# Token rows transposed by VectorE and DRAM transfers in a macaron block; sine part joined, floor moved to GpSimd

## The reference

```python
x = x + 0.5 * ffn(layernorm(x))
x = x + attn(layernorm(x))         # softmax of 0.5 + 0.2*sigmoid(qk) + 0.15*tanh(qk) + 0.1*relu(qk), over 1024 keys
x = x + 0.5 * ffn(layernorm(x))
# in ffn, for each of its 2 layers:
h = shift_token(x)                 # upper 64 features come from the token before
qkv = h @ wqkv                     # 128 -> 3 x 512
q = l2norm(q) * qs; k = l2norm(k) * ksc
q, k = rotary_xpos(q, k)           # q*cos*scale + rotate_half(q)*sin*scale
o = local_attention(q, k, v)       # windows of 64, this window and the last
x = x + o @ wo
h = layernorm(shift_token(x)) * lg + lb
a, g = split(h @ w1 + b1)
x = x + (a * gelu(g)) @ w2 + b2
```

## Time and profile before

| | |
|---|---|
| median of 3 runs | 3134.05 us (3133.75 to 3137.78) |
| the profiled execution | 3130.48 us |
| its span in the trace | 3128.7 us, granted TensorE clock 0.993 |
| TensorE matmul busy | 3019.2 us (97%) |
| VectorE busy | 2676.7 us (86%) |
| ScalarE busy | 2224.1 us (71%) |
| GpSimd busy | 1676.7 us (54%) |
| DMA queues | 107.23 MB, mean 34 GB/s |

### The profile page before, as it was taken

How to read it: one execution, slowest core, us unless ns; L and a number is a source line. 1 busy time by engine, 2 the same in 40 slices (tenths; PEclk the granted TensorE clock), 3 DMA queues, 4 the chain that set the end, 5 groups by cost and what they waited for, 6 DMA issues and landing times.

```text
span 3128.7 us, 84476 instructions
## 1 busy us (share of the span) xinstructions
PE 3019.2 (97%) x31009; PEld 2182.5 (70%) x31009; DVE 2676.7 (86%) x6052; ACT 2224.1 (71%) x5488; POOL 1676.7 (54%) x1000
## 2 busy tenths in 40 slices
PE   6999999999999999989999699999999999999999
PEld 3777777666777777656777477777766677777766
DVE  6999999678888888768999599999966888888865
ACT  4888888436888887328889388888853688888832
POOL 6888886115666665541000588888621466666610
PEclk9999999999999999999999899999999999999999
DMA  4111112101111111100000011111211111111211
GB/s 117 33 35 34 33 38 51 45 20 31 33 36 33 36 43 42 46 8 1 1 1 1 18 35 35 34 33 40 45 47 22 31 33 36 33 36 40 46 39 51
DMA packets 136855, 107.23 MB, mean 34 GB/s; under 512 B 80937, under 2 KB 102402, under 8 KB 136450
## 3 DMA queue, kind: packets, MB, share of 16 engines
q1 hardware_dynamic: 136450, 101.83, 14.4%
HBM read 12.67 MB, written 4.19 MB: 5 GB/s over the span
## 4 chain that ended last, share of the span: by engine, by line
PE 88%; DVE 8%; issue 2%; ACT 2%; DMA 0%; SPq 0%; DVEq 0%; ACTq 0%
PE psum L1171 13%; PE psum L1045 10%; PE psum L1148 7%; PE psum L1184 7%; PE psum L1195 7%; PE psum L1215 6%; PE psum L1102 6%; PE psum L1071 5%; PE psum L1136 4%; PE psum L1416 3%; PE psum L1229 3%; PE psum L1242 3%; PE psum L1392 3%; PE psum L1092 3%; PE psum L1402 2%
## 5 line engine op out<-in xcount | busy, mean ns | idle before, releaser
L420 POOL TENSOR_TENSOR rnorm<-ssq_floor,neg_half 128x16 f32<-128x16 f32 x256 | 746.7, 2917 | 659.8 <-DVE qkr L741 626.4
L495 ACT ACTIVATE shared<-psum,neg_max 128x128 f32<-128x128 f32 x2048 | 594.3, 397 | 24.5 <-DVE neg_max L717 24.5
L425 POOL TENSOR_TENSOR qk_cos<-qk_cos,qk_sin 128x1024 f32<-128x1024 f32 x256 | 607.8, 2374 | 0.0
L1171 PE MATMUL psum<-wqkv,hT 128*128 128x512 f32 x1024 | 533.9, 605 | 21.6 <-DVE qk_sin L702 9.7
L702 DVE TENSOR_TENSOR qk_sin<-psum,sin 128x256 f32<-128x256 f32 x1024 | 382.0, 414 | 90.9 <-ACT sq L502 89.9
L516 ACT COPY shared<-psum 128x512 f32<-128x512 f32 x256 | 150.0, 586 | 358.5 <-PE psum L1136 358.5
L708 DVE TENSOR_TENSOR qk_cos<-psum,cos 128x512 f32<-128x512 f32 x512 | 348.7, 682 | 55.1 <-ACT sq L502 54.9
L554 ACT ACTIVATE shared<-psum,b1g 128x512 f32<-128x512 f32 (+1 forms) x192 | 131.3, 686 | 351.7 <-PE psum L1045 349.6
L1195 PEld LDWEIGHTS psum<-wo,shared 128*128 128x128 f32 x2048 | 267.0, 192 | 139.5 <-issue 139.2
L502 ACT ACTIVATE sq<-psum 128x512 f32<-128x512 f32 x512 | 335.0, 654 | 30.9 <-PE psum L1171 30.9
L1045 PE MATMUL psum<-shared,w1g 128*128 128x512 f32 (+1 forms) x768 | 345.8, 593 | 7.2 <-DVE shared L807 5.3
(11 more groups left out here) (131 smaller groups left out, 6580.2 us busy)
## 6 DMA issues: line engine op xcount, KB each, us to landing
vprev<-v SPq DMA_DIRECT2D x512, 130.0 KB, 2.3
shared<-Y SPq DMA_DIRECT2D x32, 256.0 KB
shared<-Y SPq DMA_DIRECT2D x32, 254.0 KB
X<-in_L_attn_x SPq DMA_DIRECT2D x8, 512.0 KB, 6.9
out<-X SPq DMA_DIRECT2D x8, 512.0 KB, 3.6
wqkv<-in_L_ffn_wqkv SPq DMA_DIRECT2D x4, 768.0 KB, 4.5
w<-in_L_ffn_w SPq DMA_DIRECT2D x4, 341.0 KB
wo<-in_L_ffn_wo SPq DMA_DIRECT2D x4, 256.0 KB, 4.8
```

Of the source, the lines that this page charges most:

```text
L420: nc.gpsimd.tensor_tensor(rnorm[:], ssq_floor[:], neg_half[:], ALU.pow).then_inc(rnorm_ready, 1)
L425: nc.gpsimd.tensor_tensor(both, both, qk_sin[:, t.m % 2, :], ALU.add).then_inc(sum_ready, 1)
L495: last = nc.scalar.activation(probs[:, c * P:(c + 1) * P], bank(3 + i, (c % 4) * P, (c % 4 + 1) * P), ACT.Exp, bias=neg_max[:, c:c + 1])
L1171: nc.tensor.matmul(bank(i), hT[:, t.m * P:(t.m + 1) * P], wqkv[:, i * INNER:(i + 1) * INNER], start=True, stop=True).then_inc(qk_psum, 1)
```

## The change

For the tiles 0 to 4 of each layer nothing changes in how they come into hT. From tile 5 on TensorE and ScalarE no longer take part. VectorE transposes the 128x128 tile of Y in sixteen squares of 32, each in its place, into one of two buffers (`token_blocks`, for tile s+7 in slot s, after the moments). SyncE stores the buffer to one of four places in DRAM (tile s+6, first in slot s) and loads the squares from there into their right places in hT with four transfers of 32 partitions (tile s+5, next in slot s); both stand ahead of the `vprev` copies. TensorE's first query projection waits for these loads (semaphore `blocks_in`).

Besides, VectorE's sine part is one instruction over both halves with the halves read in reverse order, so that a tile counts 4 rotary steps instead of 6, and the floor of the sums goes from VectorE to GpSimd, ahead of its power. The wait of `scores` for hT falls away.

```diff
+def late_count(t):
+    return t.L * (64 - EARLY) + t.row - EARLY
...
+            def store_blocks(t):
+                k = late_count(t)
+                sp.wait_ge(blocks_ready, k + 1)
+                wait(sp, blocks_in[k % 4], 64 * (k // 4))
+                sp.dma_start(blocks_out[k % 4], blocks[:, k % 2, :]).then_inc(blocks_stored[k % 4], 16)
+
+            def load_blocks(t):
+                k = late_count(t)
+                sp.wait_ge(blocks_stored[k % 4], 16 * (k // 4 + 1))
+                wait(sp, v_psum, before(t, MT - 1))
+                squares = blocks_out[k % 4].rearrange("(b i) (j c) -> i b j c", i=SQUARE, c=SQUARE)
+                for j in range(P // SQUARE):
+                    lo = t.m * P + (1 if j * SQUARE >= HALF else 0)
+                    sp.dma_start(hT[j * SQUARE:(j + 1) * SQUARE, lo:lo + P].rearrange("i (b c) -> i b c", c=SQUARE),
+                                 squares[:, :, j, :]).then_inc(blocks_in[k % 4], 16)
...
             def local_slot(L, s):
+                if t := late_tile(L, s + 6):
+                    store_blocks(t)
+                if t := late_tile(L, s + 5):
+                    load_blocks(t)
                 if t := tile_at(L, s + 3):
                     wait(sp, v_ready, before(t, 0))
...
             def root(t):
-                wait(pool, floor_ready, before(t, 0))
+                wait(pool, ssq_ready, before(t, 0))
+                wait(pool, rnorm_ready, before(t, 1))
+                nc.gpsimd.tensor_scalar(ssq_floor[:], ssq[:], 1e-24, None, ALU.max).then_inc(floor_ready, 1)
+                pool.wait_ge(floor_ready, t.n + 1)
                 wait(pool, qkr_ready, before(t, 1))
...
-                if s >= 0 and (t := tile_at(L, s + 5)):
-                    tokens(t)
...
-                for e in range(2):
-                    lo = e * (DH // 2)
-                    nc.vector.tensor_tensor(
-                        y[:, :, e, :], x[:, :, 1 - e, :],
-                        sin[:, t.m, i:i + 1, lo:lo + DH // 2].to_broadcast([P, HEADS, DH // 2]),
-                        ALU.mult).then_inc(rot_ready, 1)
+                part = sin[:, t.m, i, :].rearrange("p (e d) -> p e d", e=2)
+                nc.vector.tensor_tensor(y, x[:, :, ::-1, :],
+                                        part.unsqueeze(1).to_broadcast([P, HEADS, 2, DH // 2]),
+                                        ALU.mult).then_inc(rot_ready, 1)
...
-                wait(dve, ssq_ready, before(t, 0))
-                wait(dve, rnorm_ready, before(t, 1))
-                nc.vector.tensor_scalar_max(ssq_floor[:], ssq[:], 1e-24).then_inc(floor_ready, 1)
...
+            def token_blocks(t):
+                k = late_count(t)
+                if t.L % DEPTH == 0:
+                    dve.wait_ge(ln_ready, 2 * NT * (t.L // DEPTH) + t.row + 1)
+                else:
+                    dve.wait_ge(y_ready, (t.L - 1) * NG + t.row // GROUP + 1)
+                if k > 1:
+                    dve.wait_ge(blocks_stored[(k - 2) % 4], 16 * ((k - 2) // 4 + 1))
+                nc.vector.transpose(blocks[:, k % 2, :], Y[:, t.row, :]).then_inc(blocks_ready, 1)
...
-                if t.row and (u := tile_at(t.L, t.row + 4)):
-                    wait(pe, hT_ready, before(u, 0, 2))
...
-                wait(pe, hT_ready, before(t, 0, 2))
+                if t.row < EARLY:
+                    pe.wait_ge(hT_ready, early_count(t, 0, 2))
+                else:
+                    pe.wait_ge(blocks_in[late_count(t) % 4], 64 * (late_count(t) // 4 + 1))
...
-                    tokens_transpose(tile(5))
```

More of the change, by code:

```diff
@@ L29 @@
 VU = P + 3
+SQUARE = 32
+EARLY = 5
 def rotary_tables(n):
@@ L94, in before, with early_count @@
     return times * (t.n + 1 - k)
+def early_count(t, k, times=1):
+    return times * (t.L * EARLY + t.row + 1 - k)
+def late_count(t):
+    return t.L * (64 - EARLY) + t.row - EARLY
 def macaron(nc, x_in, wq_in, bq_in, wk_in, bk_in, wv_in, bv_in, wo_att_in, bo_in,
@@ L105, in macaron @@
     NC = len(HID_CHUNKS)
-    assert MT == 8 and GROUP == 4 and N == 2 * BANK
+    assert NT == 64 and MT == 8 and GROUP == 4 and N == 2 * BANK
     x_rows = x_in.rearrange("b (m p) d -> b p m d", p=P)
     out_rows = out.rearrange("b (m p) d -> b p m d", p=P)
+    blocks_out = nc.dram_tensor("token_blocks", [4, P, P], F32).ap()
     with ExitStack() as ctx:
@@ L141, in macaron @@
         hT = sb("hT", [P, MT * P + 1])
+        blocks = sb("blocks", [P, 2, P])
         sq = sb("sq", [P, 2 * INNER])
@@ L225, in macaron @@
         h_in = [sem(f"h_in{i}") for i in range(3)]
+        blocks_ready = sem("blocks_ready")
+        blocks_stored = [sem(f"blocks_stored{i}") for i in range(4)]
+        blocks_in = [sem(f"blocks_in{i}") for i in range(4)]
         heads = lambda t: t.rearrange("p (h d) -> p h d", d=DH)
@@ L286, in x_bank, with late_tile @@
         def x_bank(t):
-            return 4 if t.row >= 5 else 1 if t.L else 6
+            return 1 if t.L else 6
+        def late_tile(L, row):
+            return tile_at(L, row) if row >= EARLY else None
         def v_bank(t):
@@ L422, in total @@
             def total(t):
-                wait(pool, rot_ready, before(t, 0, 6))
+                wait(pool, rot_ready, before(t, 0, 4))
                 both = qk_cos[:, t.m % 2, :]
@@ L504, in tokens @@
             def tokens(t):
-                wait(act, staged_T, before(t, 0))
+                wait(act, staged_T, early_count(t, 0))
                 wait(act, v_psum, before(t, MT - 1))
@@ L868, in local_slot @@
                     moments(2 * NT * (L // DEPTH) + rows[0], rows)
+                if t := late_tile(L, s + 7):
+                    token_blocks(t)
                 if s == 1:
@@ L900, in mlp_slot @@
                     keys(new)
+                if fills(L, g) and (u := late_tile(L + 1, g - NG + 7)):
+                    token_blocks(u)
                 if g % 2 == 1 and (g + 3) // 2 < NP:
@@ L1033, in gates @@
                     pe.wait_ge(w1g_ready, t.L + 1)
-                    pe.wait_ge(rot_ready, 6 * NT * (t.L + 1))
+                    pe.wait_ge(rot_ready, 4 * NT * (t.L + 1))
                 elif t.row == 0 and c == 1:
@@ L1114, in tokens_transpose @@
                 if x_bank(t) == 6:
-                    wait(pe, hT_ready, before(t, 1, 2))
-                elif x_bank(t) == 4:
-                    wait(pe, probs_ready, 2 * (t.n - 4))
+                    wait(pe, hT_ready, early_count(t, 1, 2))
                 elif u := tile_at(t.L, t.row - 3):
@@ L1120, in tokens_transpose @@
                 elif t.row:
-                    wait(pe, rot_ready, before(t, 1, 6))
+                    wait(pe, rot_ready, before(t, 1, 4))
                 elif t.L == DEPTH:
@@ L1176, in project_v @@
                 if v_bank(t) == 0:
-                    wait(pe, rot_ready, 6 * (t.n + 1) + 3)
+                    wait(pe, rot_ready, 4 * (t.n + 1) + 2)
                 elif u := tile_at(t.L, t.row - 5):
@@ L1208, in weights_transpose @@
                     elif i == 0:
-                        pe.wait_ge(hT_ready, before(tile_at(t.L, 4), 0, 2))
+                        pe.wait_ge(hT_ready, early_count(tile_at(t.L, 4), 0, 2))
                     else:
@@ L1222, in keys_transpose @@
                 if u := tile_at(t.L, t.row + 2):
-                    pe.wait_ge(rot_ready, 6 * u.n + 3)
+                    pe.wait_ge(rot_ready, 4 * u.n + 2)
                 else:
@@ L1235, in queries_transpose @@
                 if t.row < 2 and t.L:
-                    pe.wait_ge(rot_ready, 6 * (t.n + 3))
+                    pe.wait_ge(rot_ready, 4 * (t.n + 3))
                 elif u := tile_at(t.L, t.row + 1):
@@ L1288, in local_slot @@
                     weights_transpose(tile(0), 1)
-                    if t := tile(5):
-                        tokens_transpose(t)
                     if t := tile(2):
```

## The result

The changed kernel takes 3260.98 us (median of 4 runs, 3258.55 to 3263.11), the kernel before 3134.6: a ratio of 1.0401, 95% interval 1.0383 to 1.0419. The profiled execution took 3258.55 us, with a span of 3256.8 us, against 3130.48 and 3128.7. So 128.1 us were added between the two profiled executions; the forecast was 3281.

A forecast was written before the change was run, and what follows sets the result against it. TensorE was taken as the bound, at 8.28 us a slot. 3130.5 - 26 - 2 - 3 + 178 (12 stalls with clock falls) = 3277.5, and 3.6 more to the median gave 3281 us, range 3218 to 3345.

The forecast's parts named there:

- The fall of the clock: TensorE running at half clock for 4.6 us after each stall: 2.3 us each, bounds 0 and 4.6.
- B: Rival: the loads' small pieces land late in every slot, 8.2 us instead of 3.9; 3602 us, chance 0.05.
- A: Rival: SyncE's 16.13 us entry doesn't hold what follows, so the loads are never late; 3103 us, chance 0.09.
- C: Rival: VectorE's transpose takes 1.02 us behind GpSimd and becomes the bound; 3296 us, within the forecast's 0.86.
- D: Rival: the 12 stalls come without the clock's fall, 28 us less; 3253 us, within the forecast's 0.86.
- the stop: TensorE waiting for late loads in slots 50, 54 and 58: 12.5 us each, 12 times, bounds 10.3 and 15.5.
- The landing: Time from a load's issue to its arrival in hT: 3.9 us, from the 64 KB identity; lower bound 2.3.
- the issue: SyncE's queue time per DMA standing in line: some 0.64 us, for one store and four loads per tile.
- My upper bound of 485.4: Latest landing of tile 54's loads: one issue held 1.5 us and half the rotary table's slowest landing more; 15.5 us.
- hidden: GpSimd's floor, taken as 0.3 us, stands ahead of its 1.27 us wait before the power in layer 0: no cost.
- I count nothing: VectorE's transpose waiting for the store of two tiles earlier, issued two slots before: no cost.
- the 31 as forecast: Gains: 26 us from TensorE's removed transposes, 2 from VectorE's shorter loop, 3 at the starts of layers 0 and 2.

The follow-up runs named there:

- the cut kernels: Changed kernel with load_tokens' second token copy cut into 112 and 15 partitions: 3111.89 us; with the layer norm's + 1e-5 also moved to VectorE: 3099.27 us.
- the experiment that took the meeting away: Changed kernel with the second token copy cut and the layer norm's + 1e-5 on VectorE, not GpSimd: 3099.27 us, ratio 0.9897.

## Why the prediction was right, and where it was off

**Right.** The bound: TensorE's slot, with 236 x 0.11 us less in it. Measured 8.18 against 8.29 in layers 1 and 3, where I had 8.17. The place, number and cause of the stops: 12, in slots 50, 54 and 58, behind the third copy. The fall of the clock behind each: some 2 us, where I had taken 2.3. The price of the two unseen operations, from the groups by form (line, engine, operation, shapes, count, busy us, mean ns, idle): VectorE's transpose takes 298 ns, where I had 0.28 us from a pass over the same shape, and GpSimd's floor 263 ns, where I had 0.3.

```profile
L869 DVE STREAM_TRANSPOSE blocks<-Y 128x128 f32<-128x128 f32 x236 | 70.4, 298 | 0.0
...
L463 POOL TENSOR_SCALAR ssq_floor<-ssq 128x16 f32<-128x16 f32 x256 | 67.4, 263 | 192.3 <-DVE ssq L802 184.1
```

Of the rivals, B (late in every slot) is refuted by the 12 and no more; A (the entry holds nothing) by the same rows, and its price, 3103, is nearly what the cut kernels take, 3112 and 3099. C and D fell with 298 ns and with the clock at 0.50.

**Mis-sized: the stop.** From the end of the long entry to TensorE's going on I had 476.06 to 482.5, 6.4 us; measured, 474.09 to 477.81, 3.7 us. Two terms were too large. The landing: 3.9 us by the row of the identity, measured 1.7 (DMA issues: what, queue, operation, count, KB each, median us from issue to landing).

```profile
token_blocks<-blocks SPq DMA_DIRECT2D x236, 64.0 KB, 1.6
hT<-token_blocks SPq DMA_DIRECT2D x944, 16.0 KB, 1.7
```

And the issue: 0.64 us each, measured 1.79 for four, 0.45 each. Both rows that I had chosen were of DMAs with other company: the identity's 3.9 us is from the kernel's first microseconds, when the weights are loaded as well, and the `vprev` median (2.3 us), my lower bound, was the nearer row by the state of the queue. The stop was 9.94 us, under my lower bound of 10.3. In the sum: 144.7 instead of 178, 33 us too many. My upper bound of 485.4 doesn't follow from its own terms: 482.5 with 1.5 and half of 8.2 more is 488.1, a stop of 18 us and not 15.5. Nothing measured comes near either.

**Failed: "hidden" for GpSimd's floor.** I put 0.3 us into a wait of 1.27 and called it covered, and so wrote 8.17 us for all four layers. Counted in the layers that normalise, the new list is:

- before: 7.04 us of work and gaps, and 1.27 of waiting;
- the floor, with the gap behind it: +0.34;
- the one-column power: 1.38 instead of 0.58, +0.80.

That is 8.2 by this count and 8.38 in the rows; the rest are two gaps, 0.07 us ahead of the floor and 0.12 more between the addition and the 1e-5. The second term I didn't foresee. `norms` of a tile needs its sum, GpSimd's addition L471. In the state of 8.39 VectorE stands 0.80 us and begins 0.08 behind that addition's end (301.62 and 301.70; the profile names no releaser, "issue", but the code waits for `sum_ready` there), and the power, which follows the addition on GpSimd, runs into it every time. So GpSimd's lateness renews itself. It can also end: in the kernel with the sine part in halves, layer 2 had a slot of 8.73 us, three of 8.18, and then 8.38 again.

Before that state begins, another is there, in which `norms` begins 0.6 us behind the addition's end and stretches the normalisation (L491, 1.40 instead of 0.80) rather than the power. The list is then 8.19 us long, with no wait either, and TensorE at 8.18 just keeps its pace:

```profile
190.56 2.36 POOL L471 TENSOR_TENSOR qk_cos<-qk_cos,qk_sin 128x1024 f32<-128x1024 f32 x1
...
193.32 0.58 POOL L487 TENSOR_TENSOR ln_rstd<-ln_rstd,neg_half 128x1 f32<-128x1 f32 x1
194.01 1.40 POOL L491 TENSOR_SCALAR Y<-X,ln_moments,ln_rstd 128x128 f32<-128x128 f32 x1
```

What tips it can be seen in slot 20 of layer 0. VectorE's maxima, and with them `norms`, come 0.2 to 0.25 us late (218.33, where 8.18 after the one at 209.90 is 218.08); the normalisation is stretched to 1.63, GpSimd is now later by as much, and its next power is the one that `norms` meets:

```profile
218.33 1.20 DVE L783 TENSOR_TENSOR qkr<-qk_cos,rnorm 128x1024 f32<-128x1024 f32 x1
```

```profile
218.57 1.63 POOL L491 TENSOR_SCALAR Y<-X,ln_moments,ln_rstd 128x128 f32<-128x128 f32 x1
...
226.31 1.58 POOL L487 TENSOR_TENSOR ln_rstd<-ln_rstd,neg_half 128x1 f32<-128x1 f32 x1
```

There is no slack to win the 0.2 us back, and VectorE's wait for the addition grows by 0.21 us a slot until, five slots on, TensorE is reached. That fits an onset that differs from layer to layer and from kernel to kernel (slots 9 to 46); where the 0.2 us came from, no row says. Another place where my text counts on cover was right in this kernel: VectorE's wait for the store ("I count nothing") doesn't appear in the list of waits of the changed kernel. It does appear, with 19.5 us, as soon as everything goes a slot earlier.

**The sum again,** with the stops and the slots of 8.39 as measured and the 31 as forecast: 3130.5 - 31 + 14 + 144.7 = 3258.2; the profiled execution took 3258.55. The two errors had opposite signs, 33 us too many and 14 too few, so that the forecast came within 20 us is in part luck.

## What to carry to other kernels

Before a step that something waits for is put into a queue, look for the longest entry of that queue, even where it costs nothing today: its price is zero only as long as nothing urgent stands behind it, and here it went from 0 to 145 us. Here the copy of 127 partitions was worth cutting into 112 and 15. And a wait on an engine is no cover for new work there until the stretch at the new times of both engines has been counted: 0.26 us put into 1.27 us of room used it all, because what follows was moved into the way of another engine.

## What the runs showed of the hardware that I had not expected

**VectorE and GpSimd hold each other up, both ways.** A GpSimd instruction that begins beside a VectorE multiplication with two inputs in SBUF (`norms`, 128x1024) ends 0.4 to 0.7 us behind its end, however short it is: the 128x1 power takes 1.38 us instead of 0.58 (0.44 behind, 74 times in the changed kernel; beside VectorE's maxima, which read PSUM, it stays at 0.58), the 128x128 normalisation some 1.40 instead of 0.80 (0.67 to 0.69 behind). The other way round, VectorE's floor of 128x16 takes 1.02 to 1.15 us instead of 0.17 and ends with GpSimd's addition. The Trainium skill (GPSIMD Engine Reference, "1. Specifications") says that GpSimd shares its SBUF interfaces with VectorE and contends with instructions that have two inputs in SBUF or run in a two-port mode; the trace agrees for `norms`, which has two inputs in SBUF; in which mode VectorE's floor runs, no row says. That it is this port was not tested by itself: the experiment that took the meeting away also shortened GpSimd's list.

**A DMA on one engine holds the queue through the DMA behind it:** 15.8 to 17.0 us in the entry after it, in all 32 places of the changed kernel (12 of them with a stop of TensorE behind), at 16 GB/s in the one shown, and no such entry when the copy is cut in 112 and 15.

**A round trip through DRAM is cheap in a quiet queue:** 64 KB stored in 1.6 us, 16 KB in runs of 128 bytes loaded in 1.7, each from issue to landing.
